# Rows sent two units later, masks and values made in the expert stage, third attention's weights loaded a stage ahead, and a norm a unit later, in a four-layer model on one core

## The reference

```python
# L0: 8 heads of 64; then 8 experts that each choose 256 of the 2048 rows
sim = q @ k.T * scale;  x = x + softmax(sim) @ v @ Wo + bo
t = log(clip(x_n @ gate_w, eps))
for _ in range(8):
    t = t - logsumexp(t, axis=-2);  t = t - logsumexp(t, axis=-1)
vals, idx = top_k(exp(t) per expert, 256)
x = x + scatter_set(idx, vals * (x_n[idx] @ experts[e]))
# L1: one head, masked; then ternary linear layers with a scale, relu squared, a fast-weight term
x = x + softmax(where(mask == 0, -1e10, Q @ K.T) / 16) @ V
# L2: one head with biases; then two ternary layers, each on its input over its root mean square
x = x + softmax((Q + bq) @ (K + bk).T / 16) @ (V + bv)
x = x + ternary(gelu_erf(ternary(x_n, w_up)), w_down)
# L3: 16 heads of 16, masked, biases, output projection; then 8 experts of 256 rows each, gelu
```

## Time and profile before

| | |
|---|---|
| three runs | 2700.22, 2703.95, 2710.94 us, median 2703.95 |
| profiled execution | 2716.91 us, span of its records 2715.1 us |
| busy PE, DVE, ACT, POOL | 2356.1 (87%), 1630.1 (60%), 1275.1 (47%), 375.0 us (14%) |
| mean granted clock of PE | 0.894 |
| transfers | 108.33 MB, mean 40 GB/s |
| stage E0 | from about 684 to 1007 us of the span |
| C1, F1 | 1007 to about 1278, to 1422 us |
| C2, F2 | 1422 to about 1696, to 1822 us |
| A3, F3 | from 1822 us on |

### The profile page before, as it was taken

The page is one execution under the profiler, slowest core; times in us unless marked ns, Lnnn a source line. Parts: engine busy times, 40 slices in busy tenths (PEclk is TensorE's granted clock), DMA queues, the critical chain, the costliest instruction groups (busy, mean ns, idle before and its releaser), DMA issues.

```text
span 2715.1 us, 32836 instructions
## 1 busy us (share of the span) xinstructions
PE 2356.1 (87%) x12316; PEld 1227.4 (45%) x12316; DVE 1630.1 (60%) x3448; ACT 1275.1 (47%) x1732; POOL 375.0 (14%) x286
## 2 busy tenths in 40 slices
PE   8999999989555449999988999776999999999788
PEld 3323222222211037777654777562444444444377
DVE  4656666655367734352542453765788867888385
ACT  3554555555166512223522222530577655776753
POOL 0343443433034520000000000000000000000011
PEclk9999999999666568999988999885899988999888
DMA  3000000000130042200101121012110202000131
GB/s 121 5 9 5 9 9 9 9 5 9 47 129 10 14 139 92 88 6 9 53 27 51 61 73 49 5 22 84 47 28 11 34 1 36 7 32 1 61 123 67
DMA packets 63389, 108.33 MB, mean 40 GB/s; under 512 B 13516, under 2 KB 44891, under 8 KB 62203
## 3 DMA queue, kind: packets, MB, share of 16 engines
q1 hardware_dynamic: 61064, 100.85, 12.0%
q0 software_dynamic: 1536, 4.20, 0.5%
q10 hardware_dynamic: 628, 1.14, 0.2%
HBM read 87.88 MB, written 17.74 MB: 39 GB/s over the span
## 4 chain that ended last, share of the span: by engine, by line
PE 52%; DVE 12%; ACT 4%; issue 3%; DMA 3%; POOL 1%; SPq 0%; ACTq 0%; DVEq 0%; POOLq 0%
PE PS L2547 8%; PE PS L1466 7%; PE PS L2528 5%; DVE pm L2656 4%; PE PS L2490 4%; PE PS L1424 2%; PE PS L1447 2%; PE PS L1449 2%; PE PS L1448 2%; ACT dump L1094 1%; DVE ind L1139 1%; PE PS L1248 1%; PE PS L373 1%; PE PS L1257 1%; PE PS L1413 1%
## 5 line engine op out<-in xcount | busy, mean ns | idle before, releaser
L2656 DVE TENSOR_REDUCE pm<-PS 128x1 f32<-128x512 f32 x768 | 478.7, 684 | 101.0 <-PE PS L2490 100.8
L2619 ACT ACTIVATE P<-PS 128x1024 f32<-128x1024 f32 (+1 forms) x416 | 407.1, 1023 | 196.6 <-PE PS L2528 195.1
L2490 PE MATMUL PS<-Ks,Qs 49*128 49x512 f32 x768 | 307.1, 487 | 42.2 <-DMA Qs<-row 26.0
L732 ACT ACTIVATE P<-PS 128x1024 f32<-128x1024 f32 (+1 forms) x208 | 213.2, 1026 | 178.9 <-PE PS L637 167.6
L2528 PE MATMUL PS<-Qs,Ks 51*128 51x512 f32 (+1 forms) x832 | 274.1, 447 | 8.6 <-ACT P L2619 8.6
L650 PE MATMUL PS<-P,V 128*64 128x512 f32 (+1 forms) x832 | 229.0, 629 | 5.8 <-ACT P L732 5.8
L2547 PE MATMUL PS<-P,V 128*17 128x512 f32 (+1 forms) x1664 | 230.2, 626 | 0.3 <-ACT P L2619 0.3
L2528 PEld LDWEIGHTS PS<-Qs,Ks 51*128 51x128 f32 (+1 forms) x832 | 138.8, 190 | 199.7 <-ACT P L2619 145.8
L2490 PEld LDWEIGHTS PS<-Ks,Qs 49*128 49x128 f32 x768 | 135.3, 198 | 133.7 <-DVE pm L2656 89.8
L552 POOL TENSOR_TENSOR odd<-odd,P 128x1024 f32<-128x1024 f32 x64 | 160.1, 2501 | 197.3 <-ACT P L732 197.3
L1032 PE MATMUL PS<-ind,sel 128*8 128x512 bf16 (+3 forms) x288 | 102.2, 474 | 90.7 <-DVE ind L1139 75.9
(11 more groups left out here) (364 smaller groups left out, 4665.2 us busy)
## 6 DMA issues: line engine op xcount, KB each, us to landing
mi<-in_mask SPq DMA_DIRECT2D x32, 800.5 KB, 4.4
We<-in_L_ffn_w SPq DMA_DIRECT2D x16, 1024.0 KB, 7.0
Wg<-gate_rows SPq DMA_DIRECT2D x8, 1024.0 KB, 11.3
Qs<-q_parts SPq DMA_DIRECT2D x90, 64.0 KB, 2.8
Ks<-k_parts SPq DMA_DIRECT2D x24, 200.1 KB, 6.2
R<-denominators SPq DMA_DIRECT2D x32, 128.0 KB, 2.8
q_parts<-T SPq DMA_DIRECT2D x7, 512.0 KB, 2.7
k_parts<-Tk SPq DMA_DIRECT2D x6, 400.0 KB, 2.5
```

The lines of the kernel that those rows point to most:

```text
L732: e.activation(self.P[0:r, n % 4, :, :], PS[0:r, b:b + 2, :], ACT.Exp, scale=0.125).then_inc(*k.ac_exp.up(("A", n)))
L2490: m = e.matmul(PS[:, b, :], self.Qs[rows, s, pr, q0:q0 + 128], self.Ks[rows, s, pr, cs], start=True, stop=not masked)
L2619: e.activation(self.P[0:r, n % 4, :, :], PS[0:r, b:b + 2, :], ACT.Exp, scale=0.25).then_inc(*k.ac_exp.up((3, n)))
L2656: e.tensor_reduce(self.pm[:, u % 2, i, c:c + 1], PS[:, ring.of(("max", key)), :], AX.X, ALU.max).then_inc(*k.dv_max.up((3, *key)))
```

## The change

Unit 15's denominators are divided on VectorE straight out of PSUM in two halves; each half releases two of the projections. E0's head is a fixed order with three key steps before the projections, one in them and four behind the sinks. `place` is split: scaling on ScalarE is a step `scaled` early in the next unit, and GpSimd's transfer a step `send` two units later. Masks 0 to 3, V's column of ones and the 13 value steps of layer 1 lie in E0's expert part; the buffers of the expert stage are placed anew for it. The weights of C2 are loaded at F1's start, ahead of layer 3's, and only three biases at C2's. In F1 and F2 the fourth group's norm moves from rise(0) to the weave with fall(0) and rise(1). In A3 the eight row transfers are first in the list and on GpSimd's queue, V's load waits for the first query stacks, and the load of wo and the clearing of `nm` come behind.

```diff
--- before.py
+++ after.py
...
-    def tail(self):
-        return self.divide_steps(15) + self.project_steps(15)
...
-            at.wait_ge(k.dv_misc, ("On", u))
+            at.wait_ge(k.dv_misc, ("On", u, qt // 2) if u == 15 else ("On", u))
...
-        elif step == "den":
+        elif step == "den" and key[0] < 15:
...
+        elif step == "den" and key[0] == 15:
+            at.wait_ge(k.pe_misc, ("den", 15))
+            at.wait_ge(k.dv_misc, ("On", 14))
+            at.wait_ge(k.ac_misc, ("On", 15))
+            b = ring.of(("den", 15))
+            for half in range(2):
+                cs = slice(256 * half, 256 * half + 256)
+                e.reciprocal(self.R[:, cs], PS[:, b, cs]).then_inc(*k.dv_misc.up(("recip", 15, half)))
+                at.wait_ge(k.dv_misc, ("recip", 15, half))
+                e.tensor_tensor(self.On[:, 1, cs], self.On[:, 1, cs], self.R[:, cs], ALU.mult).then_inc(
+                    *k.dv_misc.up(("On", 15, half)))
+            ring.freed["den", 15] = (k.dv_misc, ("recip", 15, 1))
+        elif step == "recip" and key[0] < 15:
...
-        elif step == "norm":
+        elif step == "norm" and key[0] < 15:
...
+        self.W = scope.place("Wg", [128, 8, N], F32)
+        alias = lambda name, at, shape: k.nc.alloc_sbuf_tensor_at(name, shape, F32, offset=at)
+        rows_at, gap = keys.end + 41024, keys.end + 12864
+        self.xe = alias("xe", rows_at, [128, 8, 2, D])
+        self.yg = alias("yg", rows_at, [128, NT, D])
+        self.ye = alias("ye", rows_at + 16384, [128, 8, 2, D])
+        xT, last = alias("xeT", gap, [128, 7, 512]), alias("xeT7", rows_at + 32768, [128, 512])
+        self.xT = [xT[:, x, :] for x in range(7)] + [last[:]]
...
     def weigh_steps(self, t):
-        return ([(self, "turn", (t,))] if t else []) + [(self, "rank", (t,)), (self, "pick", (t,)),
-                                                        (self, "place", (t,))]
-
-    def expert_steps(self):
-        out = [(self, "fetch", (x,)) for x in range(8)] + [(self, "flip", (0,)), (self, "flip", (1,))]
+
+        out = [(self, "send", (t - 2,))] if t > 1 else []
+        out += [(self, "scaled", (t,))] + ([(self, "turn", (t,))] if t else [])
+        return out + [(self, "rank", (t,)), (self, "pick", (t,)), (self, "place", (t,))]
+
+    def expert_steps(self, mask):
+
+        out = [(self, "fetch", (x,)) for x in range(8)] + mask.load_steps(0, 2) + [(self.keys, "ones", ())]
+        out += [(self, "flip", (0,)), (self, "flip", (1,))]
         for x in range(8):
             out += [(self, "expert", (x,)), (self, "put", (x,))]
             if x < 6:
                 out.append((self, "flip", (x + 2,)))
-        out += [(self, "get", (t,)) for t in range(NT)]
+            if x == 4:
+                out += mask.turn_steps(0, 2) + mask.load_steps(2, 4)
+        out += [(self, "get", (t,)) for t in range(NT)] + mask.turn_steps(2, 4) + self.keys.value_steps()
         for g in range(4):
             out += [(self, "add", (t,)) for t in range(4 * g, 4 * g + 4)]
             if g < 3:
                 out += self.norms.steps(2, g)
         return out
 
-    def order(self):
+    def order(self, mask):
         sink = [(self, "sink", (i,)) for i in range(8)] + [(self, "spread", ())]
         out = [(self, "clear", ())]
-        out += weave((self.att.tail() + sink, 0.0, 1.0), (self.keys.key_steps(), 0.3, 1.0))
+        divide, project, keys = self.att.divide_steps(15), self.att.project_steps(15), self.keys.key_steps()
+        out += divide[:-1] + keys[0:3] + divide[-1:] + project[0:4] + keys[3:4] + project[4:] + sink + keys[4:]
         out.append((self, "begin", ()))
         todo = []
         for t in range(NT):
@@ -940,7 +957,7 @@
                 out.append((self, "count", (t, x)))
                 out += slots[x]
             todo = self.weigh_steps(t)
-        return [s for s in out + todo + self.expert_steps() if s]
+        return [s for s in out + todo + [(self, "send", (t,)) for t in (NT - 2, NT - 1)] + self.expert_steps(mask) if s]
...
-        elif step == "place":
+        elif step == "send":
...
-        elif step == "place":
+        elif step == "scaled":
...
         self.at = region.at
+        if biased:
+            self.V = region.place("V" + L, [128, KT, D + 1], F32)
         self.wk, self.wv, self.wq = (region.place(n + L, [128, 2, D], F32) for n in ("Wk", "Wv", "Wq"))
         self.mid = region.at
-        self.V = region.place("V" + L, [128, KT, D + 1], F32)
+        if not biased:
+            self.V = region.place("V" + L, [128, KT, D + 1], F32)
...
+    def bias_steps(self):
+        return [(self, "biases", ())]
...
-            if self.biased:
-                e.dma_start(self.bq[:], a[L + "bq"]).then_inc(*self.ld.up("bq", 16))
-                e.dma_start(self.bk[:], a[L + "bk"]).then_inc(*self.ld.up("bk", 16))
-                e.dma_start(self.bv[:], a[L + "bv"]).then_inc(*self.ld.up("bv", 16))
             for t, n in ((self.wk, "Wk"), (self.wv, "Wv"), (self.wq, "Wq")):
                 e.dma_start(t[:], a[L + n + "T"].rearrange("(h p) n -> p h n", p=128)).then_inc(*self.ld.up("all", 16))
+        elif step == "biases":
+            a, L = self.k.a, self.L
+            e.dma_start(self.bk[:], a[L + "bk"]).then_inc(*self.ld_b.up("bk", 16))
+            e.dma_start(self.bq[:], a[L + "bq"]).then_inc(*self.ld_b.up("bq", 16))
+            e.dma_start(self.bv[:], a[L + "bv"]).then_inc(*self.ld_b.up("all", 16))
...
     def gpsimd(self, e, at, step, key):
-        pass
+        k = self.k
+        if step == "ones":
+            at.wait_own(k.pl_done)
+            e.memset(self.V[:, :, D:D + 1], 1.0).then_inc(*k.pl_done.up(("V ones", self.layer)))
...
-                at.wait_ge(self.ld, "all")
+                at.wait_ge(self.ld_b, "all")
...
+    def load_steps(self, lo, hi):
+        return [(self, "load", (t,)) for t in range(lo, hi)]
+
+    def turn_steps(self, lo, hi):
+        return [(self, "turn", (t,)) for t in range(lo, hi)]
...
         t, = key
+        if step == "turn":
+            return
...
         t, = key
+        if step == "load":
+            return
...
-        rest = norms.steps(norm, 3) + self.kv.value_steps()
+        rest = norms.steps(norm, 3)
         if self.layer == 2:
-            out += self.kv.key_steps()
+            out += [(self.kv, "ones", ())] + self.kv.key_steps()
+            rest += self.kv.value_steps()
         out += self.query_steps(0) + weave((self.max_steps(0), 0.0, 1.0), (rest, 0.0, 0.9))
...
-            at.wait_own(self.k.pl_done)
-            e.memset(self.kv.V[:, :, D:D + 1], 1.0).then_inc(*self.k.pl_done.up(("V ones", self.layer)))
...
-    out = weave((ffn.rise_steps(0), 0.0, 1.0), (norms.steps(norm, 3), 0.0, 1.0))
+    out = ffn.rise_steps(0)
     for qb in range(4):
         parts = [(ffn.fall_steps(qb), 0.0, 1.0), (aside[qb], 0.0, 0.9)]
         if qb < 3:
             parts.append((ffn.rise_steps(qb + 1), 0.0, 1.0))
-        if qb:
-            parts.append((norms.steps(norm + 1, qb - 1), 0.05, 0.9))
+        parts.append((norms.steps(norm + 1, qb - 1) if qb else norms.steps(norm, 3), 0.05, 0.9))
...
-        out = [(self, "begin", ()), (self, "load", ())] + self.key_loads(0)
-        out += [(self, "part", (0, 0))] + self.query_loads(0, 0) + [(self, "rows load", ()), (self, "value load", ())]
+        out = [(self, "begin", ()), (self, "rows load", ())] + self.key_loads(0)
+        out += [(self, "part", (0, 0))] + self.query_loads(0, 0) + [(self, "value load", ()), (self, "load", ())]
...
         elif step == "value load":
+            at.wait_ge(*self.query_loaded(0, 0))
...
+        elif step == "rows load":
+            at.wait_ge(k.dv_misc, "row")
+            row, ones = self.row.row[0:1, :].bitcast(F32), self.row.row[32:34, :].bitcast(F32)
+            wide = lambda x, n: x[:, 0:n].unsqueeze(1).to_broadcast([x.shape[0], 4, n])
+            Ks, Qs = (x[:].bitcast(F32).rearrange("p s r n -> p (s r) n") for x in (self.Ks, self.Qs))
+            for o in (48, 112):
+                e.dma_start(Ks[o:o + 1, :, :], wide(row, M)).then_inc(*self.ld_row.up((o, "mask"), 16))
+                e.dma_start(Ks[o + 1:o + 3, :, :], wide(ones, M)).then_inc(*self.ld_row.up((o, "ones"), 16))
+                e.dma_start(Qs[o:o + 1, :, 0:M], wide(ones[0:1, :], M)).then_inc(*self.ld_row.up((o, "q"), 16))
+                e.dma_start(Qs[o:o + 1, :, M:N], wide(ones[0:1, :], N - M)).then_inc(*self.ld_row.up("all", 16))
...
-        elif step == "rows load":
...
-    out.append(("E0", kv1.load_steps() + gates.order()))
...
+    out.append(("E0", kv1.load_steps() + gates.order(mask1)))
...
-    out.append(("C1", att1.order(mask1.steps(0, 4), [mask1.steps(4, 10), mask1.steps(10, NT), [], []])))
+    out.append(("C1", att1.order([], [mask1.steps(4, 10), mask1.steps(10, NT), [], []])))
...
-    out.append(("F1", keys3.load_steps() + ffn1.order()))
...
+    out.append(("F1", kv2.load_steps() + keys3.load_steps() + ffn1.order()))
...
```

(2 more changed lines are left out.)

37 lines of the change are left out of this document (11 added, 26 removed).

## The result

The changed kernel takes 2634.8 us in the median of four runs (2620.8 to 2640.4), the kernel before 2705.4 in the same comparison: ratio 0.9731, 95% interval 0.9686 to 0.9776. Run again beside the kernel before, six runs gave 2633.0 us and 0.9729 (0.9693 to 0.9764). That is 70 us less, where the text forecast 92; 2634.8 lies in the range of 2592 to 2638, near its upper end. The two profiled executions differ by 86 us in their spans (2715.1 and 2629.0), and the difference between 86 and 70 needs an explanation too.

What follows compares the result with a forecast made beforehand. PE's matmul time was taken to bound most of the span, with gains only where PE stands still; −10 − 9.5 − 36.5 − 14 − 8 − 3 − 11.5 = −92.5 from 2703.95 gave 2612 us, range 2592 to 2638.

Steps and rivals of the forecast that it cites:

- A: A0's last division: PE's 14.73 us wait for the denominators' round trip shortens, first sink earlier; −10 us (−8.5 to −12).
- A2: Sinks: four key steps leave the chain and lie behind the last sink; −9.5 us (−4 to −9.9).
- B: Count loop: DVE's 39.5 us wait for POOL's adds goes, about 3 us staying; −36.5 us (−22 to −40).
- C: Masks and values moved from C1 into the expert stage: −7.9, −7.5 and +1.3, together −14 us (−17 to −11).
- D: C2's start: with its weights already there, PE's 11.76 us wait shortens; −8 us (−10.5 to −6).
- E: Norm a unit later: F2's rise(0) shortens by some 9 us, the next unit pays +5 to +6; −3 us (−6 to +3).
- F: A3's start: row loads on POOL first, query store landing in 7.5 us, first maximum earlier; −11.5 us (−8.4 to −16).
- the first: Rival: in the count loop sends stop DVE or POOL in turn, gaining 22 for 36.5; 2626 us, chance 0.11.
- The second: Rival: A3's store runs as freely as others once V is out of the way, −16 there; 2607 us, chance 0.07.
- The third: Rival: the count loop's slack goes to PE at a low clock, −25 there; 2626 us, chance 0.06.
- The fourth: Rival: A3's row loads on POOL cost a descriptor per element, about 400 us; slower, 2993 us, chance 0.02.
- The fifth: Rival: the late send still waits for DVE's `pick`, count loop gains under 10; 2639 us, chance 0.05 with smaller gains.

## Why the prediction was right, and where not

Right in its sign, in its places and, as a range, in its size; 22 us too large at its centre. By its steps:

- **A** was sized at −10 and gave −7. The start of the projections was right (11.5 us after the denominators; the reciprocals took 1.76 us for an estimated 1.6). The step that failed is the stretch behind it, from the projection to the first sink, which I put at 11.8 us for 17.0, "with one key step fewer between". Three fewer lay in it, and it took 15.1: one key step stayed ahead of the statistics on DVE, and the gate matmuls ran at 1.2 GHz, 3.56 us for 1.85.
- **A2** −9.5, measured −9.3. Its cover held: 1.0 to 1.5 us came back behind the last sink.
- **B** −36.5, measured −35.4 and −34.7. The reason given was right, DVE's wait for POOL's adds, but that the number came so near is partly luck. I had read the waits from 786 us on, 39.5 us, and let 3 of them stay. Over the whole loop they were 46.6 us and 6.0 stayed, so 40.6 went; and DVE's own work, for which I had no term, grew by 5.2 us. I also priced the two links as one. The runs show that the delayed send alone does it, and that the part of the change that scales early costs 2 us.
- **C** was forecast at −14 and gave −6 to −8: the masks −7 to −8 as worked out; the values mostly 5 for 7.5. I took the phase of maxima to shrink by all of their time, as PE bound it. Without them PE stood still longer there, 5.0 us for 3.8, and its clock was 0.70 to 0.81 for 0.93 with them in the experiment (0.78 and 0.80 before the change); how much each has of the gap isn't shown. The price was off as well: I had read four matmuls as two value steps, and they are one, so at 1.02 us for four the 52 matmuls would have been worth 13 us. That 7.5 is near 5 is luck. The first gather came 4.4 and 4.8 us later after the last compare, for 1.3. The way to the last expert's copy, for which I had counted SP's order of issue and DVE's masks, is 1.6 us of the 4.4; the other 2.8 are the last store, and for the transfer engines that masks and stores share I had no term.
- **D** −8, measured −7.5 (the gap went from 11.8 to 4.1 us). The loads cost F1 nothing.
- **E** −3, measured −3.
- **F** −11.5, measured −7.9, outside its own bounds of −8.4 to −16 by half a microsecond. The issue of the eight rows went as said. The step that failed is that the store shares the engines "only with the key stacks" and takes 7.5 us: I had put the rows beside it at no price, they went ahead of it into the place that V left, and it took 11.15. With the rows out of its way it took 6.4.
- **The clock in F1** had no term, and F1 took 7 us more in most traces. The text allowed ±8 us for A3's clock alone. That 2634.8 lies in the range owes as much to the range's width as to the sum.

Of the rivals, the first (sends stop DVE) is refuted in its size by sends of 1.01 us that land as fast as before, and by 6 us of waits. VectorE's operations here held no descriptor back by an amount that shows, so what the Trainium skill (page "SBUF — State Buffer", section "🔬 SBUF: two separate sides") warns of did not decide here. The test is narrow: the first ten of the sixteen sends were issued beside the compare with its sum (L1158), and the next four, which began beside plain compares and small operations, took 1.00 to 1.07 us. But the two engines did slow each other, by way of POOL's adds, which grew by 8.3 us, and DVE's small operations, which grew by 11. The second (the store runs freely) fell with the 11.1 us. The third fell: PE's clock in the loop rose, from 0.63 to 0.71. The fourth: eight issues of 0.5 to 0.6 us, nowhere near one per element. The fifth fell with the 35 us.

## What to carry to other kernels

When a wait ends with the last link of a chain of several engines, take each link out by itself before the gain is put down to one: here the late send was worth all of it and the early scaling, on top, less than nothing. When a transfer is moved out of another's way, look at what is issued ahead of it next; a small transfer put first can cost as much as the large one that left. Work taken from a phase that TensorE bounds can be worth less than its time, 5 us for 7.5 here: TensorE stood still longer in what was left of the phase and ran at a lower granted clock there. And when a wait has gone, look at the length of the operations that are now run side by side: here GpSimd's adds lengthened VectorE's small operations by 11 us in the loop.
